# Attention weights of an edge stage: seven chunks packed on 32 partitions, per-chunk work eleven steps behind the front

## What is computed

```python
h = relu(layernorm(x))
x_l, x_r = h @ W_l + b_l, h @ W_r + b_r          # (N, 4, 32)
m = leaky_relu(x_l[s] + x_r[d], 0.2)             # s, d: edges and self loops
e = einsum('ehc,hc->eh', m, att)                 # one score per edge and head
e = exp(e - segment_max(e, d)[d])
alpha = e / segment_sum(e, d)[d]
x = x + segment_sum(alpha * x_l[s], d) + bias
```

## Time and profile before

| | us |
|---|---|
| median of three runs (3007.73 to 3014.38) | 3010.88 |
| span of the profiled execution | 3004.5 |
| busy: DVE / PE / ACT / POOL | 2446.2 / 2407.2 / 2216.2 / 1901.2 |
| stage a, from its first statistics to the first instruction of stage b | 458.96 to 1490.86 |

### The profile page before, as it was taken

The page is one execution under the profiler, slowest core; times in us unless marked ns, Lnnn a source line. Parts: engine busy times, 40 slices in busy tenths (PEclk is TensorE's granted clock), DMA queues, the critical chain, the costliest instruction groups (busy, mean ns, idle before and its releaser), DMA issues. The chain is left out here.

```text
span 3004.5 us, 59828 instructions
## 1 busy us (share of the span) xinstructions
PE 2407.2 (80%) x16674; PEld 1696.9 (56%) x16674; DVE 2446.2 (81%) x6275; ACT 2216.2 (74%) x4901; POOL 1901.2 (63%) x1629
## 2 busy tenths in 40 slices
PE   6999988988988888887677777777777777397877
PEld 4666664544444444444355565555555555387776
DVE  7878777999998999987788888887888887376665
ACT  6988887898888888887566565655655655298887
POOL 2546777777777777777367787777877777500000
PEclk9999999999999999999899999999999999799999
DMA  7999984444443444443356666666666666789997
GB/s 241 296 302 295 294 271 142 150 145 137 150 147 131 149 149 133 149 131 129 102 115 122 123 122 116 123 115 117 124 109 122 123 113 120 202 344 426 426 411 301
DMA packets 365038, 556.92 MB, mean 185 GB/s; under 512 B 140129, under 2 KB 216405, under 8 KB 339779
## 3 DMA queue, kind: packets, MB, share of 16 engines
q1 hardware_dynamic: 268050, 447.47, 45.0%
q0 software_dynamic: 96880, 108.25, 18.6%
HBM read 323.07 MB, written 241.15 MB: 188 GB/s over the span
## 5 line engine op out<-in xcount | busy, mean ns | idle before, releaser
L672 POOL DMA_INDIRECT sum_dram<-b_sum,b_at x392 | 639.6, 1632 | 190.5 <-issue 93.7
L588 POOL DMA_INDIRECT a_xs<-in_x,index x352 | 354.0, 1006 | 114.5 <-issue 105.0
L597 POOL DMA_INDIRECT a_xd<-in_x,index x352 | 357.7, 1016 | 107.3 <-issue 97.2
L1481 PE MATMUL bank<-b_rows,b_same 128*128 128x128 bf16 x4704 | 291.3, 224 | 0.0
L1117 ACT ACTIVATE d_n<-d_x,stat_d_shift,stat_d_rstd 128x128 f32<-128x128 f32 x686 | 283.8, 487 | 0.2 <-DVE stat_d_shift L708 0.2
L1514 PE MATMUL bank<-wo,f_ssp_out 128*128 128x128 f32 x1568 | 227.0, 291 | 70.6 <-DVE f_ssp_out L1063 69.1
L606 POOL DMA_INDIRECT x_dram<-a_xo,index x196 | 219.7, 1121 | 90.2 <-issue 57.0
L1481 PEld LDWEIGHTS bank<-b_rows,b_same 128*128 128x128 bf16 x4704 | 276.4, 100 | 0.0
L660 POOL DMA_INDIRECT x_dram<-b_xo,sidx x196 | 221.6, 1131 | 78.6 <-issue 68.9
L1514 PEld LDWEIGHTS bank<-wo,f_ssp_out 128*128 128x128 f32 x1568 | 202.6, 202 | 88.7 <-DVE f_ssp_out L1063 82.5
L1305 PE MATMUL bank<-ident,d_n 128*128 128x128 f32 x1184 | 191.6, 287 | 68.5 <-DMA d_n<-sum_dram 37.3
(11 more groups left out here) (192 smaller groups left out, 6668.5 us busy)
## 6 DMA issues: line engine op xcount, KB each, us to landing
d_x<-in_x SPq DMA_DIRECT2D x196, 256.0 KB
x_dram<-d_x SPq DMA_DIRECT2D x196, 256.0 KB
out<-d_x SPq DMA_DIRECT2D x49, 1024.0 KB, 10.4
sum_dram<-zero SPq DMA_DIRECT2D x48, 1024.0 KB, 5.7
d_x<-x_dram SPq DMA_DIRECT2D x45, 1024.0 KB, 14.3
d_n<-sum_dram SPq DMA_DIRECT2D x25, 1024.0 KB, 11.8
x_end_dram<-a_xo SPq DMA_DIRECT2D x98, 256.0 KB
b_x<-x_end_dram SPq DMA_DIRECT2D x98, 256.0 KB
```

What stands on the lines that cost most here:

```text
L588: pool.indirect_dma_start(a_xs[t % DEPTH][:, j * F:(j + 1) * F], None, x, column(t, j)).then_inc(gathered[t % GSEM], 16)
L597: pool.indirect_dma_start(a_xd[t % DEPTH][:, j * F:(j + 1) * F], None, x, column(t, TILES + j)).then_inc(gathered[t % GSEM], 16)
L672: pool.indirect_dma_start(sum_dram, bass.IndirectOffsetOnAxis(ap=b_at[s][:, j:j + 1], axis=0), b_sum[s][:, j * F:(j + 1) * F], None, compu ...
L1481: last = pe.matmul(bank[6][:, i * F:(i + 1) * F], b_same[s][:, j, i * P:(i + 1) * P], b_rows[s][:, part, j * F:(j + 1) * F], start=(j == 0 ...
```

## The change

The scores of seven chunks are collected on 32 partitions (eight per head: seven chunks and one spare) in one bank of PSUM, by score products whose 32 weight columns are shifted by one for each chunk (`mine`). Once in seven steps a *pack* is worked off in four phases, the first four steps after its last chunk: what each row would carry to the next is found first (`tails`, `tail_sums`, `tail_logs`, a 32x32 product `same_head`, `carry_max`, `carry_den`, `carry_in`), then the softmax runs once over 32x512 (`run_max`, `run_den`, `shares`) and gives `p_beta`. In the back of a chunk a product with `pick` spreads its four rows of `p_beta` over 128 partitions, with the sign turned. VectorE makes `a_gate` and `a_pv` from it and scans the sum directly into `a_o`.

The back of chunk c moves from step c+2 to step c+11 (`LAG`). Values are kept in the slot of `a_xs`, which is therefore left later (`weighted`), as is `a_xd` (`x1_ready`). The difference of turned target and source rows is taken on VectorE (`a_dif`) and `neg_wl` goes. Statistics are taken four chunks ahead rather than three. POOL's gathers are spread over 79 chunks rather than 90; its other code and `EARLY` stay. The lists of stage d gain a scan and some small tables on VectorE, two more small stores on POOL and a 32x896 mask (not shown below). The buffer and semaphore lists are left out too.

```diff
+PACK = 7
+PR = 32
+LAG = 11
+LEAD = 4
...
+BY_DVE = {"max": 3, "sum": 4, "own": 6, "dif": 9, "den": 11, "q": 17, "dec": 18, "scan": 19, "beta": 20}
+BY_ACT = {"score": 1, "tail": 2, "log": 3, "ratio": 4, "lse": 5, "abs": 6, "down": 7, "decayed": 8, "up": 9, "den_log": 10, "rec": 11}
...
+            def pack_rows(b):
+                s = b % 2
+                if b >= 2:
+                    sp.wait_ge(rows_dve, by_dve(b - 2, "dec"))
...
+                for h in range(HEADS):
+                    rows = bass.AP(tensor=keep_dram.tensor, offset=PACK * b * C, ap=[[C, 8], [1, C + 1]])
+                    sp.dma_start(p_keep[s][8 * h:8 * h + 8, :], rows).then_inc(pack_loaded[s], 16)
+                    sp.dma_start(p_last[s][8 * h:8 * h + 8, :], last_dram[PACK * b:PACK * b + 8, :]).then_inc(pack_loaded[s], 16)
...
             def step_a(t):
...
+                if t % PACK == 2 and t < NC:
+                    pack_rows(t // PACK)
+                c = t - LAG + 1
+                if 0 <= c < NC:
...
+                        sp.wait_ge(weighted, c - 1)
...
-                        pool.wait_ge(norm_src, t - DEPTH + 1)
+                        pool.wait_ge(weighted, t - DEPTH + 1)
...
-                    pool.wait_ge(norm_dst, t - DEPTH + 1)
...
+                until = min(len(rest), -(-len(rest) * (t + 1) // (NC - LAG - 8)))
                 for gather, g, h in rest[done:until]:
                     gather(g, h)
                 done = max(done, until)
...
+            def row(ins, b, n):
+                ins.then_inc(rows_dve, 1)
+                dve.wait_ge(rows_dve, 20 * b + n)
...
+            def tails(b):
+                dve.wait_ge(rows_act, by_act(b, "score"))
+                dve.wait_ge(pack_loaded[b % 2], 128 * (b // 2 + 1))
...
+                row(dve.tensor_tensor(p_tail[:, 0:C], p_score[:, :], p_last[b % 2][:, 0:C], ALU.add), b, 1)
+                row(dve.tensor_reduce(p_col[:, 0:1], p_tail[:, :], mybir.AxisListType.X, ALU.max), b, 2)
+                dve.tensor_scalar(p_col[:, 1:2], p_col[:, 0:1], -1.0, None, ALU.mult).then_inc(rows_dve, 1)
+            def tail_sums(b):
+                dve.wait_ge(rows_act, by_act(b, "tail"))
+                dve.tensor_reduce(p_col[:, 2:3], p_tail[:, :], mybir.AxisListType.X, ALU.add).then_inc(rows_dve, 1)
+            def tail_logs(b):
+                dve.wait_ge(rows_act, by_act(b, "log"))
...
+            def carry_max(b):
+                w = whole[:, PACK * b:PACK * b + PACK]
+                dve.wait_ge(row_mm, b + 1)
...
+            def carry_den(b):
+                dve.wait_ge(rows_act, by_act(b, "ratio"))
...
+            def carry_in(b):
+                dve.wait_ge(rows_act, by_act(b, "lse"))
...
+            def run_max(b):
+                row(dve.tensor_tensor_scan(p_run[:, 1:C + 1], p_score[:, :], p_keep[b % 2][:, 1:C + 1], p_run[:, 0:1], ALU.max, ALU.mult), b, 16)
+                dve.tensor_tensor(p_q[:, :], p_score[:, :], p_run[:, 0:C], ALU.subtract).then_inc(rows_dve, 1)
+            def run_den(b):
+                dve.wait_ge(rows_act, by_act(b, "down"))
+                dve.scalar_tensor_tensor(out=p_dec[:, :], in0=p_dec[:, :], scalar=1.0, in1=p_keep[b % 2][:, 0:C],
...
+                dve.wait_ge(rows_act, by_act(b, "decayed"))
+                dve.wait_ge(rows_dve, by_dve(b, "dec"))
+                dve.tensor_tensor_scan(p_run[:, 0:C], p_dec[:, :], p_tail[:, 0:C], 0.0, ALU.mult, ALU.add).then_inc(rows_dve, 1)
+            def shares(b):
+                dve.wait_ge(rows_act, by_act(b, "rec"))
+                if b >= 2:
+                    dve.wait_ge(spread, PACK * (b - 1))
+                dve.scalar_tensor_tensor(out=p_beta[b % 2][:, :], in0=p_up[:, :], scalar=1.0, in1=p_run[:, 0:C],
...
+                c = t - LAG
+                back = 0 <= c < NC
+                front = t < NC
+                b = t // PACK - 1
+                phase = t % PACK
+                packed = 0 <= b < NC // PACK
+                if front:
+                    dve.wait_ge(h_dst, t + 1)
+                    dve.wait_ge(turned_src, t + 1)
...
+                    dve.tensor_tensor(a_dif[:, :], a_hd[t % (LAG + 1)][:, :], bank[0][:, :], ALU.subtract).then_inc(differed, 1)
                 if back:
...
+                    s = c % 2
+                    dve.wait_ge(spread, c + 1)
...
+                    dve.scalar_tensor_tensor(out=a_gate[:, :], in0=bank[7][:, :], scalar=1.0, in1=a_keep[s][:, :],
...
+                    dve.tensor_tensor(a_pv[:, :], bank[7][:, :], a_xs[c % DEPTH][:, :], ALU.mult).then_inc(weighted, 1)
+                    dve.wait_ge(weighted, c + 1)
...
+                    dve.tensor_tensor_scan(a_o[s][:, :], a_gate[:, :], a_pv[:, :], a_o[1 - s][:, C - 1:C] if c else 0.0,
+                                           ALU.mult, ALU.add).then_inc(sum_scan, 1)
+                if packed and phase == 0:
+                    tails(b)
+                if packed and phase == 1:
+                    tail_logs(b)
+                if packed and phase == 2:
+                    carry_in(b)
+                if packed and phase == 3:
+                    run_den(b)
+                if front:
+                    dve.wait_ge(v_copied, t + 1)
...
+                    dve.scalar_tensor_tensor(out=a_u[:, :], in0=bank[2][:, :], scalar=cols[:, 3:4], in1=a_xs[t % DEPTH][:, :],
...
+                if packed and phase == 1:
+                    carry_max(b)
+                if packed and phase == 2:
+                    run_max(b)
+                if t + LEAD < NC:
+                    sums_a(t + LEAD)
+                if back:
+                    dve.wait_ge(out_turned, c + 1)
+                    if c >= 4:
+                        dve.wait_ge(end_stored[s], 16 * ((c - 4) // 2 + 1))
+                        dve.wait_ge(early_scattered[s], 16 * EARLY[s] * ((c - 4) // 2 + 1))
+                    dve.tensor_tensor(a_xo[c % 4][:, :], bank[6][:, :], a_xd[c % DEPTH][:, :], ALU.add).then_inc(x1_ready, 1)
+                if t % 2 and t + LEAD < NC:
...
+                if t % 2 == 0 and t + 2 < NC:
...
+                if packed and phase == 0:
+                    tail_sums(b)
+                if packed and phase == 1:
+                    carry_den(b)
+                if packed and phase == 3:
+                    shares(b)
+            for t in range(LEAD):
+                sums_a(t)
+                if t % 2:
...
+            for t in range(NC + LAG):
                 step_a(t)
...
+                b = t // PACK - 1
+                phase = t % PACK
+                packed = 0 <= b < NC // PACK
                 if front:
...
                     act.wait_ge(turned_dst, t + 1)
...
+                    if t >= LAG + 1:
+                        act.wait_ge(based, t - LAG)
+                    act.activation(a_hd[t % (LAG + 1)][:, :], bank[1][:, :], ACT.Relu).then_inc(h_dst, 1)
+                if packed and phase == 0:
+                    act.wait_ge(score_mm, PACK * (b + 1))
...
+                        act.wait_ge(rows_dve, by_dve(b - 1, "q"))
+                    act.activation(p_score[:, :], bank[5][0:PR, :], ACT.Copy).then_inc(rows_act, 1)
+                if packed and phase == 1:
+                    act.wait_ge(rows_dve, by_dve(b, "sum"))
+                    act.activation(p_col[:, 3:4], p_col[:, 2:3], ACT.Ln).then_inc(rows_act, 1)
+                if packed and phase == 2:
+                    act.wait_ge(rows_dve, by_dve(b, "den"))
+                    act.activation(p_den[:, 0:PACK], p_den[:, 0:PACK], ACT.Ln).then_inc(rows_act, 1)
                 if ahead:
                     norms_src(t + 1)
...
                 if front:
                     act.wait_ge(self_mm, t + 1)
...
                     act.activation(a_us[:, :], bank[2][:, :], ACT.Relu, bias=cols[:, 3:4]).then_inc(self_relu, 1)
...
                     act.wait_ge(v_mm, t + 1)
...
+                    act.activation(a_xs[t % DEPTH][:, :], bank[3][:, :], ACT.Copy).then_inc(v_copied, 1)
+                if packed and phase == 0:
+                    act.wait_ge(rows_dve, by_dve(b, "max"))
+                    act.activation(p_tail[:, :], p_tail[:, :], ACT.Exp, bias=p_col[:, 1:2]).then_inc(rows_act, 1)
+                if packed and phase == 3:
+                    act.wait_ge(rows_dve, by_dve(b, "scan"))
+                    act.activation(p_run[:, 0:C], p_run[:, 0:C], ACT.Ln, bias=1.0).then_inc(rows_act, 1)
+                    act.wait_ge(rows_act, by_act(b, "den_log"))
+                    act.activation(p_run[:, 0:C], p_run[:, 0:C], ACT.Exp, scale=-1.0).then_inc(rows_act, 1)
                 if ahead:
                     norms_dst(t + 1)
+                if t % 2 and t + LEAD < NC:
...
+                if packed and phase == 1:
+                    act.wait_ge(rows_dve, by_dve(b, "dif"))
...
+                if packed and phase == 2:
+                    act.wait_ge(rows_dve, by_dve(b, "q"))
+                    act.activation(p_tail[:, 0:C], p_q[:, :], ACT.Abs).then_inc(rows_act, 1)
```

(94 more changed lines are left out.)

264 lines of the change are left out of this document (113 added, 151 removed).

## The result

The changed kernel takes 3076.2 us (median of four runs, 3072.3 to 3086.1) where the kernel before took 3011.4: the ratio is 1.0231 (interval 1.0206 to 1.0257). The profiled execution went from a span of 3004.5 to 3070.4 us, +65.9.

| stretch | before | after | difference | predicted |
|---|---|---|---|---|
| setup and node stage, to the first statistics | 459.0 | 470.5 | +11.5 | +3 |
| to the first scatter | 35.1 | 102.1 | +67.0 | +56 |
| stream, to the end of the last gather | 942.9 | 894.4 | -48.5 | -67 |
| to the first instruction of the next stage | 53.9 | 116.1 | +62.2 | +58 |
| the two stages behind | 1513.6 | 1487.3 | -26.4 | 0 |

What follows compares the result with a forecast made beforehand. POOL (GpSimd) was taken to bound the edge stage. Start +59, stream -67 and end +58 sum to +50 us on the 3004.5 us span, 3054.5; the median lies 6.4 higher, so 3061 us, range 3015 to 3108.

Steps and rivals of the forecast that it cites:

- What bounds: Edge stage: POOL (GpSimd), full with indirect transfers, sets the pace; VectorE runs ahead until the four `a_xo` buffers are used.
- Start of the stream: From the setup to POOL's first scatter in the edge stage: it comes at 553 us, +59 us.
- The front-only steps: Steps 1 to 10 of the edge stage, without a back part: 6.0 us each, bounds 5.3 to 8.9.
- The stream: POOL's first scatter to its last gather: 670 transfers at 1.308 us, 876 us (851 to 912) against 942.9, -67 us.
- the excess: Time per POOL transfer above the undisturbed 1.272 us, seen with two-SBUF-input VectorE operations: 0.091 us, scaled to 0.038.
- Removed waits: POOL's gathers drop one wait and one semaphore step a chunk: worth nothing, as the gap is 0.30 us before every kind.
- The engines' step: Mean edge-stage step of the engines other than POOL: 9.7 us, against 11.1 us for POOL's transfers.
- After the last gather: Last gather to the next stage's first instruction: 112 us (80 to 130) where 53.9 stood, +58 us.
- The stages behind: The stages after the edge stage: they see no changed instruction, 0 us.
- The engines did not become the bound: Rival, edge stage: pack's chain or TensorE's clock pushes the mean step over POOL's 11.1 us; 3130 at 12 us; chance 0.15.
- The short steps did not run at the 3.1 us: Rival, ten start and fifteen end steps: they run at TensorE's pace, 49 us less, 3012 us; chance 0.10.
- VectorE was not the bound: Rival, edge stage: VectorE was the bound and POOL follows; 1.8 us a step, some 150 us, goes, 2860 us; chance 0.03.

## Why the prediction was right, step by step

**What bounds.** Right. GpSimd never waits between 573 and 1477 us, and delaying it alone, by 24.6 us, moves the end of its stream by 20.5. VectorE's 97% in the earlier trace rows was the second bound, 0.8 us a chunk below: that is what 9.70 with half the gathers against 10.5 with all of them shows.

**Start of the stream**, +59 said, +78.6 measured (553 against 572.6); two terms were too small. Up to the first statistics it is 11.5 instead of 3, beyond the bound of 6: I counted VectorE's added operations and not the added stores. The one of 4-byte pieces delays two others by 7 to 8 us. With it moved, some 6 us of the difference went, within a spread as large; the rest stays open. The front-only steps took 6.7 instead of 6.0, inside their bounds of 5.3 to 8.9; a value nearer the whole step of the earlier trace rows would have been the better choice, since ScalarE stands between the products. `a_u` of chunks 0 and 8:

```profile
488.30 0.75 DVE L1053 SCALAR_TENSOR_TENSOR a_u<-bank,cols,a_xs 128x512 f32<-128x512 f32 x1 [3.61 <-ACT a_xs L1321]
...
541.71 0.75 DVE L1053 SCALAR_TENSOR_TENSOR a_u<-bank,cols,a_xs 128x512 f32<-128x512 f32 x1 [1.67 <-ACT a_xs L1321]
```

These two make some 15 of the 20 us. Another 2 lie between the first statistics and the first `a_u`, which the prediction kept as it was (17.8 us, 15.9 before), and the last 2 in the steps of the first pack and step 11.

**The stream**, -67 said, -48.5 measured: 1.335 a transfer instead of 1.308, within the bounds of 851 to 912. The mechanism held and the scaling failed. I scaled the excess with the share of time that two-input operations cover. The sum scan stayed one a chunk, but 47 of 82 transfers begun in it were long, where 28 of 91 were before, and what these have beyond 0.95 us each rose from 17 to 29 us. That the scan meets the transfers in another pattern once VectorE waits for scatters is likely and was not tried alone. Of the 48.5 us only some 19 come from faster transfers; the other 29 are 22 scatters that now lie behind the last gather, 158 ahead of it instead of 180.

**Removed waits.** Right: the gap in front of each kind is still 0.30.

**The engines' step**, 9.7 said, 9.46 measured. The size is right, from single runs with half of the gathers. I made it of TensorE's 8.9 us and waits in the pack's chain. Such waits are small there, as TensorE is busy 97% of the time: 9.14 us a chunk at a granted clock of 0.96, where the kernel before took 8.77 at 1.00.

**After the last gather**, +58 said, +62.2 measured, 116.1 against 112. What is missing is TensorE's granted clock, which the sum left out. The chain of a short step was priced at 4.9 us, and a step does take that at full clock; where TensorE is granted half of it (1.2 of 2.4 GHz), a step takes 6.8. Two steps of the changed kernel, and the last six of the run with the store moved:

```profile
1560.33:1565.24 4.91, 3.52 (x20) 2.32 (x21) 3.26 (x5) 0.00 (x0) 2.54 (x2) 1.00 0.26 88
1571.06:1577.84 6.78, 6.48 (x19) 4.10 (x19) 3.26 (x4) 0.00 (x0) 1.95 (x2) 0.50 0.15 53
```
```profile
1541.02:1581.68 40.66, 39.02 (x114) 25.14 (x114) 19.58 (x24) 0.00 (x0) 11.78 (x12) 0.50 0.21 67
```

In the changed kernel's own profile the last six steps took 34.6 us, at a mean of 0.69, where 29 were priced. In three other profiles they all stand at 0.50 and take 40.7, which is 6 of the 7 us by which those ends are longer.

**The stages behind**, 0 said, -26.4 measured. "No changed instruction" was true and not enough, since the tensors that they read had moved. Without this gift the difference is some +92, which the range would still have held (3102.7).

**Rivals.** The engines did not become the bound: no wait of GpSimd for `a_xo` in the stream. The short steps did not run at the 3.1 us that the prediction gave TensorE: at full clock it was busy 3.5 of 4.9 us, and only at half clock did it fill them, 6.5 of 6.8. And VectorE was not the bound: its busy share fell by a quarter and the time didn't follow. The errors partly cancelled: 20, 19 and 4 us too little at the start, in the stream and at the end, against 26 of unforeseen gain, leave the 16 by which +50 fell short of +66. That the total came so near is in part luck.

## What to carry to other kernels

An engine whose instructions follow one another at a fixed gap, here 0.30 us, is full, whatever its busy share says; delay its first instruction alone, and if the end moves by nearly as much, it is the bound, and work taken off the other engines mostly turns into waiting. A deeper software pipeline is paid at both ends of the loop, here some 130 us for nine steps more, so weigh that against the saving of the whole loop and against the engine that comes next. When a stage with the same code changes its time, look at where its tensors lie before looking for a cause in the program.

## What the hardware showed that was not expected

Moving some DRAM tensors by 106496 bytes changes a stage of 1128 us by 19 us, and by 21 us the other way in the other kernel. A store of 98 pieces of 4 bytes lands after 10.6 us and holds up two stores behind it by 7 to 8 us. The same short step took 4.9 us at TensorE's full clock and 6.8 at half. And moving one input of a VectorE scan from SBUF to PSUM, which does nothing for VectorE, makes another engine's stream 29 us shorter.
